# Graph transformer layers: gathers of last ranks, a zero fill and VectorE passes moved between edges and nodes

## The reference

```python
def gt_layer(x, ntype, etype, src, dst, Wk, Wq, Wv, Wa, Watt, Wmsg, pri, skip, g, b):
    k, q, v = (typed_linear(x, ntype, W).reshape(n, H, HS) for W in (Wk, Wq, Wv))
    kw = einsum('nhd,htdo->nhto', k, Watt)[src, :, etype]
    m = einsum('nhd,htdo->nhto', v, Wmsg)[src, :, etype]
    a = einsum('ehd,ehd->eh', kw, q[dst]) * pri[:, etype].T / SQRT_D
    att = edge_softmax(a, dst, n)
    hag = segment_sum((m * att[:, :, None]).reshape(-1, H * HS), dst, num_segments=n)
    h = silu(typed_linear(hag, ntype, Wa))
    alpha = sigmoid(skip[ntype])[:, None]
    return layernorm(h * alpha + x * (1.0 - alpha)) * g + b
```

## Time and profile before

| | us |
|---|---|
| median of 3 runs | 7626.15 |
| lowest and highest | 7616.61, 7626.69 |
| the profiled execution | 7647.14 |
| its span | 7645.3 |
| table blocks, first to last product | 516.9 to 1077.9; 3947.6 to 4543.4 |
| edges, first to last edge gather | 1090.6 to 3775.1; 4554.4 to 7236.9 |
| merge blocks, first instruction | 3800.1; 7261.6 |

### The profile page before, as it was taken

How to read it: one execution, slowest core, us unless ns; L and a number is a source line. 1 busy time by engine, 2 the same in 40 slices (tenths; PEclk the granted TensorE clock), 3 DMA queues, 4 the chain that set the end, 5 groups by cost and what they waited for, 6 DMA issues and landing times. The chain is left out here.

```text
span 7645.3 us, 75934 instructions
## 1 busy us (share of the span) xinstructions
PE 4035.8 (53%) x19359; PEld 3020.6 (40%) x19360; DVE 3561.3 (47%) x6703; ACT 1677.7 (22%) x4065; POOL 3805.7 (50%) x3900
## 2 busy tenths in 40 slices
PE   0128865555555555555448875555555555555514
PEld 0113334444444444444423334444444444444414
DVE  1215544444444444444456654444444444444446
ACT  0015531111111111111136651111111111111115
POOL 0542235555555555555513345555555555555454
PEclk9569986666666666666668986666666666666656
DMA  3149964444444444444438974444444444444420
GB/s 69 39 140 378 401 246 139 139 140 139 139 139 139 140 140 140 140 139 138 140 143 357 375 284 140 136 143 138 136 139 140 139 139 139 139 139 139 133 53 29
DMA packets 404617, 1224.31 MB, mean 160 GB/s; under 512 B 162025, under 2 KB 215277, under 8 KB 354392
## 3 DMA queue, kind: packets, MB, share of 16 engines
q0 software_dynamic: 200944, 852.07, 33.5%
q10 hardware_dynamic: 56448, 218.59, 7.7%
q1 hardware_dynamic: 147104, 152.21, 7.3%
HBM read 576.25 MB, written 718.61 MB: 169 GB/s over the span
## 5 line engine op out<-in xcount | busy, mean ns | idle before, releaser
L1008 POOL DMA_INDIRECT kv_e<-table_d,row_s x1568 | 1504.9, 960 | 1190.2 <-issue 817.2
L1008 POOL DMA_INDIRECT kv_e_<-table_d,row_s_ x1568 | 1507.9, 962 | 1183.5 <-issue 814.6
L1143 PE MATMUL qe_ps<-q_w,of_rank 128*128 (+1 forms) x3168 | 629.4, 355 | 686.7 <-issue 639.2
L1143 PE MATMUL qe_ps_<-q_w_,of_rank_ 128*128 (+1 forms) x3168 | 622.1, 351 | 670.7 <-issue 592.0
L1143 PEld LDWEIGHTS qe_ps<-q_w,of_rank 128*128 128x128 f32 x3168 | 538.3, 254 | 721.4 <-issue 720.6
L1143 PEld LDWEIGHTS qe_ps_<-q_w_,of_rank_ 128*128 128x128 f32 x3168 | 531.2, 251 | 700.7 <-issue 699.4
L1177 PE MATMUL sum_ps_<-pv_,to_rank_ 128*128 128x136 f32 x3136 | 602.7, 376 | 156.7 <-DVE pv_ L1095 156.7
L1177 PE MATMUL sum_ps<-pv,to_rank 128*128 128x136 f32 x3136 | 601.5, 375 | 148.8 <-DVE pv L1095 148.8
L1177 PEld LDWEIGHTS sum_ps_<-pv_,to_rank_ 128*128 128x128 f32 x3136 | 583.5, 280 | 185.0 <-issue 185.0
L1177 PEld LDWEIGHTS sum_ps<-pv,to_rank 128*128 128x128 f32 x3136 | 582.2, 279 | 177.1 <-issue 177.1
L1057 DVE TENSOR_TENSOR to_rank<-lane,local_c 128x512 f32<-128x512 f32 x396 | 255.4, 686 | 650.3 <-remote 576.9
(11 more groups left out here) (376 smaller groups left out, 6538.5 us busy)
## 6 DMA issues: line engine op xcount, KB each, us to landing
part_d<-sums ACTq DMA_DIRECT2D x98, 1088.0 KB
part_d<-sums_ ACTq DMA_DIRECT2D x98, 1088.0 KB
local_b<-local_d SPq DMA_DIRECT2D x100, 512.0 KB
local_b_<-local_d SPq DMA_DIRECT2D x100, 512.0 KB
kv_e<-table_d,row_s POOLq DMA_INDIRECT x1568
kv_e_<-table_d,row_s_ POOLq DMA_INDIRECT x1568
q_w<-q_d SPq DMA_DIRECT2D x100, 64.0 KB
q_w_<-q_d SPq DMA_DIRECT2D x100, 64.0 KB
```

The lines of the kernel that those rows point to most:

```text
L1008: pool.indirect_dma_start(out=kv_e[:, b, t, :], out_offset=None, in_=table_d, in_offset=bass.IndirectOffsetOnAxis(ap=row_s[:, b, t:t + 1], ...
L1143: last = pe.matmul(qe_ps[:, t * D:(t + 1) * D], of_rank[:, b, t, :], rows, start=True, stop=True)
```

## The change

- A store of zeros is added in the first block: the rows of `part_d` of the last group of 112 tiles, for all 128 ranks.
- `part_l`, its semaphore and the gather become shared by the edges and the merge. Behind its loop over the chunks GpSimd waits for the stores of chunks 0 to 90 and issues the gathers of groups 0 to 12. Group 13's stays in the merge block. The tile now lives until the next table block (layer 0) or the end.
- In the merge VectorE's product over `h_sb` moves behind three passes over `through` and `into`, ahead of the wait for ScalarE's copies.
- In layer 1 VectorE clears `w_buf` as its first instruction of the merge, in place of GpSimd behind the copies.
- In the table block of layer 1 `up.clear` comes ahead of the clearing of `h_t` and `edge_w`.

```diff
@@ first block, SP @@
+            sp.dma_start(part_d.rearrange("(j t) f -> j t f", t=ET)[:, (NG - 1) * GT:ET, :],
+                         zero[:, 0:REC].unsqueeze(1).broadcast_to([P, GT, REC])).then_inc(s_out, 16)
             sp.dma_start(info_d.rearrange("(k p) f -> p k f", p=P), absent[:]).then_inc(s_out, 16)
             sp.dma_start(local_d[EP:EP + 2 * CT * P].rearrange("(a b) -> a b", b=P), zero_bf[0:2 * CT, :]).then_inc(s_out, 16)
-            sp.wait_ge(s_out, 16 * (4 + QDUMP // P + 3))
+            sp.wait_ge(s_out, 16 * (4 + QDUMP // P + 4))
@@ table block, VectorE @@
+                if up:
+                    up.clear(dve)
                 dve.memset(h_t[:], 0.0)
                 dve.memset(edge_w[:], 0.0).then_inc(s_zero, 1)
                 if up:
-                    up.clear(dve)
@@ edges @@
+        ends = ExitStack()
+        part_l = sb(ends, "part_l", [GT, NG, REC])
+        s_last = sem("c_last")
+
+        def gather_last(pool, g):
+            pool.indirect_dma_start(out=part_l[:, g, :], out_offset=None, in_=part_d,
+                                    in_offset=bass.IndirectOffsetOnAxis(ap=last_i[0:GT, g:g + 1], axis=0)).then_inc(s_last, 16)
@@ edges, GpSimd, behind the loop @@
+                early = (NG - 1) * GT // CT
+                for b in range(2):
+                    pool.wait_ge(s_out[b], ONE + 16 * len(range(b, early, 2)))
+                for g in range(NG - 1):
+                    gather_last(pool, g)
@@ merge, GpSimd @@
-                for g in range(NG):
-                    pool.indirect_dma_start(out=part_l[:, g, :], out_offset=None, in_=part_d,
-                                            in_offset=bass.IndirectOffsetOnAxis(ap=last_i[0:GT, g:g + 1], axis=0)).then_inc(s_last, 16)
+                gather_last(pool, NG - 1)
                 if l == L - 1:
+                    pool.wait_ge(s_zero, 1)
                     pool.wait_ge(s_copy, NG)
-                    pool.memset(w_buf[:], 0.0).then_inc(s_zero, 1)
-                    pool.wait_ge(s_zero, 1)
                     for k in range(XEARLY):
@@ merge, VectorE @@
+                if l == L - 1:
+                    dve.memset(w_buf[:], 0.0).then_inc(s_zero, 1)
                 dve.tensor_tensor(hot[:], lane[:, 0:NT].unsqueeze(1).broadcast_to([P, NS, NT]),
...
-                dve.wait_ge(s_gate, 6)
-                dve.tensor_tensor(h_sb[:], h_sb[:], nd.rest[:].unsqueeze(2).broadcast_to([P, NS, D]), ALU.mult)
+                if l == L - 1:
+                    dve.wait_ge(s_zero, 1)
                 dve.wait_ge(s_load, 64)
...
                 dve.tensor_scalar(through[:], through[:], BIG, -BIG, ALU.mult, ALU.add).then_inc(s_v, 1)
+                dve.wait_ge(s_gate, 6)
+                dve.tensor_tensor(h_sb[:], h_sb[:], nd.rest[:].unsqueeze(2).broadcast_to([P, NS, D]), ALU.mult)
                 dve.wait_ge(s_v, 3)
                 dve.wait_ge(s_copy, NG)
```

More of the change, by code:

```diff
@@ L948, in program @@
         lay.close()
+        if l:
+            ends.close()
+        ends = ExitStack()
[4 more added lines that the diff above has]
+                                    in_offset=bass.IndirectOffsetOnAxis(ap=last_i[0:GT, g:g + 1], axis=0)).then_inc(s_last, 16)
         st = ExitStack()
@@ L1189, in program @@
         part_f = sb(st, "part_f", [GT, NG, REC])
-        part_l = sb(st, "part_l", [GT, NG, REC])
         part_m = sb(st, "part_m", [GT, NG, 2 * H])
@@ L1204, in program @@
         with nc.Block() as block:
-            s_load, s_last, s_wide, s_turn, s_copy, s_v, s_exp, s_back, s_rec, s_out, s_w, s_skip, s_gate, s_x, s_zero = (
-                sem("c_" + n) for n in ("load", "last", "wide", "turn", "copy", "dve", "exp", "back", "rec", "out", "w", "skip", "gate", "x", "zero"))
+            s_load, s_wide, s_turn, s_copy, s_v, s_exp, s_back, s_rec, s_out, s_w, s_skip, s_gate, s_x, s_zero = (
+                sem("c_" + n) for n in ("load", "wide", "turn", "copy", "dve", "exp", "back", "rec", "out", "w", "skip", "gate", "x", "zero"))
             @block.gpsimd
             def _(pool):
-                for g in range(NG):
-                    pool.indirect_dma_start(out=part_l[:, g, :], out_offset=None, in_=part_d,
-                                            in_offset=bass.IndirectOffsetOnAxis(ap=last_i[0:GT, g:g + 1], axis=0)).then_inc(s_last, 16)
+                gather_last(pool, NG - 1)
                 if l == L - 1:
+                    pool.wait_ge(s_zero, 1)
                     pool.wait_ge(s_copy, NG)
-                    pool.memset(w_buf[:], 0.0).then_inc(s_zero, 1)
-                    pool.wait_ge(s_zero, 1)
                     for k in range(XEARLY):
```

## The result

The changed kernel took **7638.65 us** (median of 17 runs, 7629.59 to 7650.99), the kernel before 7621.6 (17 runs, 7608.7 to 7626.69). The ratio is 1.0025, 95% interval 1.0017 to 1.0032: about 17 us slower. The forecast was 7617.6 in a range up to 7632, and slower by over 0.2% had a chance of 0.09.

The account below looks back on a forecast made before the run. No engine was busy for more than 53% of the span, so the change was read stage by stage. Terms -15.0 - 15.3 - 3.9 - 3.0 + 28.7 = -8.5 us gave 7617.6 us for the median, range 7603 to 7632.

Parts of the forecast that it names:

- Part 1: End of edges, both layers: thirteen gathers fit GpSimd's 24.79 us of idle; cost 0, up to 16.3 us each without that cover.
- with the block starting no later after the last edge gather: Expected sign at the end of the edges: thirteen gathers in the 25 us before the merge do not delay its start.
- Rival D: End of edges: gathers don't fit or move; held to 3 us each by VectorE, 14 us per layer, net +20; chance 0.03.
- Part 2: Merge, layer 0: copies start at 3811.2 instead of 3826.25, SP loads late next; gain 15.0 us, bounds 11 and 20.
- C: Merge, both layers: rival that copies wait for SP's whole queue; gains of 11 us each, net -0.2; chance 0.09.
- part 3: Merge, layer 1: copies start at 7272.5 instead of 7287.81, VectorE's clearing hidden by 0.4 us; gain 15.3 us, bounds 11 and 16.
- were the one gather held behind the clearing, it would be issued by 7269: Merge, layer 1: case of the remaining gather held behind VectorE's clearing; claimed it would still be in time.
- Part 4: Merge, layer 1: without GpSimd's clearing the x gathers start 7.0 us earlier; gain 3.9 us, bounds 3.9 and 7.0.
- Part 5: Table block, layer 1: first aggregate gather moves up as gather buffers are cleared first; gain 3.0 us, bounds 1.5 and 3.3.
- Part 6: Preparation: zero store of part_d, 14336 packets at 500 per us, all on the path; cost 28.7 us, bounds 24.7 and 32.
- A: Preparation: rival that the zero store is cheap, 414 GB/s, 20.0 us; net -17.2, 7609 us; chance 0.14.
- B: Preparation: rival that the zero tile limits the store to 140 GB/s, 59 us; net +21.8, 7648 us; chance 0.06.

Follow-up runs that it names:

- e1: The changed kernel with all 14 last-rank gathers back in the merge block; one run, 7641.45 us (kernel before on that chip 7622.7).
- e14: The changed kernel with zero store in the third preparation block, ScalarE clearing w_buf, gathers split 4, 6 and 4; 7594.26 against 7625.21 us before, ratio 0.9966.
- e9: The changed kernel with layer 1's w_buf cleared by ScalarE instead of VectorE; one run, 6269.39 us (kernel before on that chip 6289.4).
- e8: The kernel before, with GpSimd waiting for the previous chunk's turn in score_t before each chunk's third quarter of gathers; ratio 1.0004.
- e3: e1 with GpSimd clearing part_l 8 times at the end of the edges; one run, 7687.83 us (kernel before on that chip 7679.0).
- e5: e1 with 13 plain SP transfers from part_d into part_l at the end of the edges; one run, 7696.05 us (kernel before there 7679.0).
- e16: The kernel before with two GpSimd waits per chunk, for the previous chunk's last sum and for its turn; ratio 1.2328.
- e4: The changed kernel with the 13 early gathers waiting for VectorE's last product; one run, 7650.95 us (kernel before on that chip 7622.7).

## Why the prediction was wrong

**Part 1, thirteen gathers at nothing: the step that failed.** "13 take 16.3 us, inside the 24.79 us of idle": they did fit, at 0.92 to 1.23 us each, and GpSimd was idle again 18 us before the next block. The step asked whether the gathers wait for anything and whether anything on GpSimd's queue waits for them. It did not ask what a stream of gathers does to the others. Its own sign for this, "with the block starting no later after the last edge gather", failed. In place of 0 it cost 10.2 and 10.7 us, on chips where TensorE's semaphores are held (e1 takes it away, e14 avoids it); on the chip of e9 it cost 0.4 and 0.2 against e8, so there the forecast of nothing was nearly right. The evidence was in the trace of before: of the copies of a turn in layer 0 all but one released by "remote", 3.1 us behind a last gather at the median.

**Rival D** had the right place, the right sign and the wrong way: it looked for gathers slowed to 3 us by VectorE. At a chance of 0.03 it could not carry the result.

**Part 2, merge of layer 0:** -14.6 for -15.0. SP's loads are late next, as said: the first copy at 11.3 behind the block's start for 11.1, released by `through`. The packet counts behind this were a little off: the microsecond from 3811 held 21 packets of 6272 B, 96 of 2048 B and 16 of 4 B, not 14 and 119, which moves the end of `through` by 0.1 us. C falls: the copies did not wait for the whole queue.

**Parts 3 and 4, merge of layer 1:** -15.6 for -19.2. Of the 3.6 missing 3.4 lie in part 3 (the copy came 11.9 us earlier, not 15.3), which had the case ("were the one gather held behind the clearing, it would be issued by 7269") and put its end too early: the gather was held for 8.80 us, beyond the clearing's 6.14, and the copy that waits for its rows came 2.9 us later than in e9. e9 shows the cause by taking VectorE's clearing away: 108.4, and 18.2 us of gain against e8's 126.6; e14 shows the same on a chip with the hold, 109.3. Part 4 held: from the first copy to the block's end 100.6 us before and 97.0 after, 3.7 for 3.9. By the rule that the prediction took from the Trainium skill ("SBUF — State Buffer", "Who interferes with whom"), that a tensor_tensor keeps GpSimd only from reading, it would have been 7.0, and the measurement decides against that sum. A gather also reads its row numbers (`last_i`, `node_i`) from SBUF, and whether it is this read that waits no run here shows.

**Part 5:** -2.9 for -3.0.

**Part 6, the zero store:** 26.9 for 28.7. It ran at 522 to 525 packets per us where the sum took 500, so 14336 packets take 27.4 us. With rows of 544 B its lower bound of 24.7 becomes 23.3, A's 20.0 becomes 18.8 and B's 59 becomes 56; the 28.7 went by packets and stays. A falls: 287 GB/s over 20 us, not 414, nor the 425 that the Trainium skill ("DMA: Bandwidth & Descriptors", "Bandwidth") gives for a transfer of 16 MB into SBUF, which no run here made. B falls too: the zero tile was no limit.

With part 1 at 0 the sum would have been -6.2 by what was measured, for the -8.5 forecast. Of the forecast's six terms four were right within 2 us.

## What to carry to other kernels

An engine's idle time is free only if what is put there leaves the others alone. Before filling it, look at the same kind of instruction elsewhere in the same trace, and at what waits beside it: a wait that ends with nothing ("remote") and nearly always the same time behind a neighbour's last instruction is a coupling that no semaphore in the code shows. Where such work must go in, cut it into pieces that end before the next result is due, and measure on more than one chip.

## What was not expected of the hardware

- On three chips (12, 0 and 2) TensorE's semaphores come late, turns by up to 13.6 us, while GpSimd issues indirect gathers and TensorE runs its sums; on a fourth (1) all turns come within 0.02 us. The same kernel takes 7619 to 7679 us there and 6289 here, and nearly all of it lies in the edge loops (2680 and 2020 us a layer). What differs between the chips stays open, and so does the mechanism. The runs show that it is not GpSimd's clearing (e3), not plain transfers of SP (e5) and not a stream's length alone (e16); that the sums inside a stream start it was seen, not tried by itself.
- Whether the changed kernel is faster without the hold was not measured. By the stages of e9 and e8 (+26.8 preparation, +0.4 and +0.2 ends, -14.4, -2.6) and layer 1's merge at 15.3, it would be 5 us, 0.1%.
- In the edges' block GpSimd's drain ends 6.1 to 7.6 us behind its last instruction on these three chips, be it a gather (e4) or a clearing (e3); in the merge block of layer 0 it was 2.2 us in the kernel before and 5.5 in the changed one. Why was not tested.
- A gather issued 0.9 us ahead of VectorE's memset of 6.14 us took 8.80 us; beside ScalarE's pass of the same size gathers took 0.93 us (e14).
